# A four-layer graph network on one core: the deep slots of the first tile in units of their own, and gather rounds of four units

## What is computed

```python
# layer 0, twice: GAT, 4 heads of 32
h = (x @ W).reshape(N, H, C)
e = leaky_relu(alpha_s[src] + alpha_d[dst], 0.2)
e_exp = exp(e - segment_max(e, dst)[dst])
out = segment_sum(h[src] * (e_exp / segment_sum(e_exp, dst)[dst])[:, :, None], dst) + bias
# layer 1: weighted neighbour sum (edge weights), two dense branches
feat_neigh = segment_sum(edge_val[:, None] * feat_in[edge_col], edge_row)
# layer 2: graph transformer, 8 heads of 16, softmax over the edges of each node,
# two batch norms and a feed-forward part
w = einsum('ehd,ehd->eh', q[e_dst], k[e_src])
# layer 3: edge MLP with two batch norms over all edges, mean over each node's edges
e = (x_dst - x_src) @ theta_w.T + x_src @ phi_w.T
e = relu(_bn(e)); e = relu(_bn(e @ fc1_w.T))
x = relu(segment_sum(e, dst) / cnt + h)
```

## Time and profile before

| | us |
|---|---|
| median of 3 runs | 11876.77 (11870.55 to 11889.13) |
| the profiled execution | 11906.11 |
| its span | 11904.2 |
| PE busy | 3666.8 (31%) |
| DVE busy | 6743.4 (57%) |
| ACT busy | 1475.4 (12%) |
| POOL busy | 7495.3 (63%) |

### The profile page before, as it was taken

How to read it: one execution, slowest core, us unless ns; L and a number is a source line. 1 busy time by engine, 2 the same in 40 slices (tenths; PEclk the granted TensorE clock), 3 DMA queues, 4 the chain that set the end, 5 groups by cost and what they waited for, 6 DMA issues and landing times. The chain is left out here.

```text
span 11904.2 us, 90167 instructions
## 1 busy us (share of the span) xinstructions
PE 3666.8 (31%) x14212; PEld 2427.7 (20%) x14213; DVE 6743.4 (57%) x12448; ACT 1475.4 (12%) x2895; POOL 7495.3 (63%) x7840
## 2 busy tenths in 40 slices
PE   2212333332224555655000000005211111113987
PEld 1211222222112333433000000002111111112433
DVE  6455677774556777765556666655322222224877
ACT  1000111110000111111000000000000000002976
POOL 4676777775767777743677777770476777773023
PEclk7556666665567887877555555557555555556998
DMA  2255444453386667673374444450236433335866
GB/s 59 69 75 94 104 105 110 111 115 62 88 96 162 183 180 189 184 165 106 100 96 115 111 111 111 111 105 2 68 105 92 105 105 105 105 105 128 288 235 216
DMA packets 928522, 1422.47 MB, mean 119 GB/s; under 512 B 191108, under 2 KB 723306, under 8 KB 927992
## 3 DMA queue, kind: packets, MB, share of 16 engines
q0 software_dynamic: 277904, 662.94, 28.4%
q10 hardware_dynamic: 549664, 498.96, 14.6%
q1 hardware_dynamic: 100680, 257.93, 6.5%
HBM read 1064.18 MB, written 355.03 MB: 119 GB/s over the span
## 5 line engine op out<-in xcount | busy, mean ns | idle before, releaser
L819 POOL DMA_INDIRECT ring<-gat_table,index x3640 | 3475.2, 955 | 1261.6 <-issue 1046.9
L819 POOL DMA_INDIRECT ring<-b_table,index x1820 | 1734.2, 953 | 678.3 <-issue 526.0
L819 POOL DMA_INDIRECT ring<-kv_table,index x1820 | 1729.5, 950 | 601.4 <-issue 526.6
L961 PE MATMUL pairs<-hot_lo,hot_hi 128*128 128x128 f32 x6272 | 1089.5, 341 | 929.0 <-PEq L959 926.0
L961 PEld LDWEIGHTS pairs<-hot_lo,hot_hi 128*128 128x128 f32 x6272 | 1002.7, 246 | 1047.5 <-issue 1017.0
L1904 DVE TENSOR_TENSOR tb<-bt,att 128x1792 f32 x130 | 263.2, 2025 | 1676.1 <-DVEq L107 1676.1
L1926 PE MATMUL bt<-ident,ring 128*128 128x128 f32 x1820 | 417.4, 421 | 1945.5 <-PEq L107 1945.5
L954 PE MATMUL pairs<-nil 128*128 128x512 bf16 x784 | 328.9, 466 | 1918.3 <-PEq L107 1789.6
L935 DVE TENSOR_SCALAR hot_lo<-ramp,lo,col 128x128 f32<-128x128 f32 x3136 | 873.2, 355 | 0.0
L714 PE MATMUL tp<-ident,stage 128*128 128x128 f32 x196 | 49.0, 427 | 2460.2 <-DVEq L701 2426.0
L2059 ACT ACTIVATE r<-kept_ring,coef 128x448 f32<-128x448 f32 x1040 | 762.6, 758 | 190.5 <-ACTq L107 166.3
(11 more groups left out here) (410 smaller groups left out, 6879.9 us busy)
## 6 DMA issues: line engine op xcount, KB each, us to landing
kept_ring<-kept SPq DMA_DIRECT2D x260, 896.0 KB, 4.7
dense_weights<-dstage ACTq DMA_DIRECT2D x392, 512.0 KB
layer_out<-dense_weights ACTq DMA_DIRECT2D x98, 1568.0 KB
kept<-tb ACTq DMA_DIRECT2D x132, 896.0 KB, 3.8
ring<-gat_table,index POOLq DMA_INDIRECT x3640
ring<-kv_table,index POOLq DMA_INDIRECT x1820
ring<-b_table,index POOLq DMA_INDIRECT x1820
col<-turned ACTq DMA_DIRECT2D x400, 32.0 KB
```

What stands on the lines that cost most here:

```text
L819: pool.indirect_dma_start(self.ring[:, r * UG + i, :], None, self.table, bass.IndirectOffsetOnAxis(self.index[:, half, at:at + 1], 0)).the ...
L961: mm = pe.matmul(self.ps[:, b, i * P:(i + 1) * P], self.hot_hi[:, u, 4 * b + i, :], self.hot_lo[:, u, 4 * b + i, :], start=False, stop=Fal ...
```

## The change

The first band is only as deep as its tiles two to seven need. What the first tile has beyond that stands in *tail units* of 14 slots of that tile alone, ahead of the first band. `tail_units` reads their number, `tail_depth` the place in the slot tables where they begin. Every pass gains a loop over them with its own form of the computation (`tail_scores`, `tail_unit`, `tail_exponent`, and a `fold` in the mean). The total is rounded up to a multiple of four, and all loops go in rounds of four units. The slot tables are longer by the number of edges and split into four groups of 32 partitions instead of three. The diff, cut; the rest of it repeats these parts for the other consumers and renumbers their loops.

```diff
-SCOLS = UMAX * UG + 8 * CH * B7
-SPARTS = ((0, 44), (44, 88), (88, P))
+SCOLS = E + UMAX * UG + 8 * CH * B7
+SPARTS = ((0, 32), (32, 64), (64, 96), (96, P))
...
+            c(dve.tensor_copy(level[:, :], band[:, :]))
+            c(dve.tensor_reduce(level[:, 0:1], md[:, 1:B7], AX.X, ALU.max))
+
+            c(dve.tensor_scalar(bi[:, :], level[:, :], float(S - 1), None, ALU.add))
             c(dve.tensor_single_scalar(bi[:, :], bi[:, :], 1, ALU.arith_shift_right))
             c(dve.tensor_scalar(bcnt[:, :], bi[:, :], float(B7), None, ALU.max))
+            c(dve.tensor_scalar(tail[:, 1:2], bcnt[:, 0:1], float(S), None, ALU.mult))
+            c(dve.tensor_tensor(tail[:, 0:1], md[:, 0:1], tail[:, 1:2], ALU.subtract))
+            c(dve.tensor_scalar(tail[:, 0:1], tail[:, 0:1], 0.5 * (UG - 1), 1.0 / UG, ALU.add, ALU.mult))
+            c(dve.tensor_scalar(tail[:, 0:1], tail[:, 0:1], WHOLE, WHOLE, ALU.add, ALU.subtract))
+            c(dve.tensor_scalar(tail[:, 0:1], tail[:, 0:1], 1.0, None, ALU.max))
+            c(dve.tensor_copy(k.total[:, 5:7], tail[:, :]))
             c(dve.tensor_tensor_scan(run[:, :], k.ones[:, 0:NB], bcnt[:, :], 0.0, ALU.mult, ALU.add))
-            c(dve.tensor_scalar(ti[:, 0:1], run[:, NB - 1:NB], 1.0, None, ALU.add))
+            c(dve.tensor_tensor(run[:, :], run[:, :], tail[:, 0:1].broadcast_to([P, NB]), ALU.add))
+            c(dve.tensor_scalar(ti[:, 0:1], run[:, NB - 1:NB], float(RU - 1), None, ALU.add))
             c(dve.tensor_single_scalar(ti[:, 0:1], ti[:, 0:1], 2, ALU.arith_shift_right))
             c(dve.tensor_copy(k.total[:, 1:2], ti[:, 0:1]))
-            c(dve.tensor_scalar(k.total[:, 0:1], ti[:, 0:1], 4.0, 2.0, ALU.mult, ALU.add))
-            c(dve.tensor_scalar(k.total[:, 2:3], ti[:, 0:1], 2.0, 1.0, ALU.mult, ALU.add))
+            c(dve.tensor_scalar(k.total[:, 0:1], ti[:, 0:1], float(RU), None, ALU.mult))
+            c(dve.tensor_scalar(k.total[:, 2:3], ti[:, 0:1], float(RU // 2), None, ALU.mult))
...
+                if w == 0:
+                    c(dve.tensor_scalar(lone[:, :], ok, float(DUMMY), None, ALU.add))
+                    dve.sem_inc(lone_ready, 1)
...
+            depth = tail_depth(k, act)
+            act.wait_ge(cleared, 1)
+            for j, (lo, hi) in enumerate(SPARTS):
+                act.dma_start(slot_src[j][:, ds(band_chunks(act, 0) * CH, CH)], blank[lo:hi, 0:CH]).then_inc(lone_out, 16)
+            act.wait_ge(lone_out, 16 * len(SPARTS))
...
+                    if first:
+                        at = ((n - i - 1) * CH).with_bounds(min_val=0, max_val=SCOLS - CH)
+                        for j, (lo, hi) in enumerate(SPARTS):
+                            act.dma_start(slot_src[j][:, ds(at, CH)], lone[lo:hi, :]).then_inc(lone_out, 16)
...
-        last = self.rounds(pool)
-        round_(0)
-        with pool.Fori(0, last):
+        with pool.Fori(0, self.rounds(pool)):
+            round_(0)
             round_(1)
-            round_(0)
...
-    def load_index(self, sp, half, unit):
+    def load_index(self, sp, half, unit, depth):
         for j, (lo, hi) in enumerate(SPARTS):
-            sp.dma_start(self.index[lo:hi, half, :], self.slots[j][:, ds(unit * UG, 2 * UG)]
+            sp.dma_start(self.index[lo:hi, half, :], self.slots[j][:, ds(depth + unit * UG, 2 * UG)]
                          ).then_inc(self.i_sem[half], 16)
...
-        round_(0, 0, RU)
         with sp.Fori(0, last) as i:
+            round_(0, i, (RU * i + RU).with_bounds(min_val=0, max_val=UMAX))
             round_(1, i, (RU * i + RU + 2).with_bounds(min_val=0, max_val=UMAX))
-            round_(0, i + 1, (RU * i + 2 * RU).with_bounds(min_val=0, max_val=UMAX))
...
+            def tail_unit(u):
+                claim(dve, ga.landed)
+                got = ga.unit(u)
+                for f in tail_scores(dve, got, e_tail[:, 0:UG, :], work):
+                    c(f())
+                top = newmax[:, 0:heads]
+                c(dve.tensor_reduce(top, e_tail[:, :, :].rearrange("p s h -> p h s"), AX.X, ALU.max))
+                dve.tensor_tensor(x_tail[:, :, :], e_tail[:, :, :], top.unsqueeze(1).broadcast_to([P, UG + 1, heads]),
+                                  ALU.subtract).then_inc(e_ready, 1)
+                claim(dve, p_ready)
+                for half, dst in ((0, first), (1, second[:, :, :])):
+                    part = slice(half * B7, (half + 1) * B7)
+                    ins = dve.tensor_tensor(by_head(dst), by_head(got[:, part, 0:VB]),
+                                            p_tail[:, part, :].unsqueeze(3).broadcast_to([P, B7, heads, dim + 1]),
+                                            ALU.mult)
+                ins.then_inc(ga.used, 1)
+                c(dve.tensor_tensor(by_head(acc[:, 0:1, :]), by_head(acc[:, 0:1, :]),
+                                    p_tail[:, UG:UG + 1, :].unsqueeze(3).broadcast_to([P, 1, heads, dim + 1]), ALU.mult))
+                c(dve.tensor_tensor(first, first, second[:, :, :], ALU.add))
+                c(dve.tensor_reduce(second[:, 0, :], first.rearrange("p w c -> p c w"), AX.X, ALU.add))
+                c(dve.tensor_tensor(acc[:, 0, :], second[:, 0, :], acc[:, 0, :], ALU.add))
+                c.reset()
...
+                if isinstance(b, int):
+                    with dve.Fori(0, tail_units(k, dve)) as u:
+                        tail_unit(u)
...
+            with act.Fori(0, tail_units(k, act)):
+                tail_exponent()
...
+                    c(dve.memset(acc[:, 1, :], 0.0))
+                    with dve.Fori(0, tail_units(k, dve)):
+                        unit(1)
+                    claim(dve, tail.summed, 2)
+                    dve.sem_inc(tail.summed, 2)
+                    c(dve.tensor_reduce(fold[:, :], acc[:, 1, :].rearrange("p (w c) -> p c w", w=B7), AX.X, ALU.add))
+                    c.reset()
+                    dve.sem_inc(tail.folded, 1)
```

More of the change, by code:

```diff
@@ L512, in _, with band @@
                 act.sem_inc(turned_out[w], 32)
-            with act.Fori(0, NB) as b:
+            depth = tail_depth(k, act)
[3 more added lines that the diff above has]
+            act.wait_ge(lone_out, 16 * len(SPARTS))
+            act.sem_inc(lone_out, -16 * len(SPARTS))
+            def band(b, first):
                 n = band_chunks(act, b)
@@ L533, in _ @@
                     act.sem_inc(written, 1)
-            total = act.value_load(k.total[0:1, 0:1], min_val=2, max_val=UMAX)
-            act.wait_ge(cleared, 1)
+            band(0, True)
+            with act.Fori(1, NB) as b:
+                band(b, False)
+            total = act.value_load(k.total[0:1, 0:1], min_val=RU, max_val=UMAX)
             for j, (lo, hi) in enumerate(SPARTS):
-                act.dma_start(slot_src[j][:, ds(total * UG, 2 * CH)], blank[lo:hi, :]).then_inc(last, 16)
+                act.dma_start(slot_src[j][:, ds(depth + total * UG, 2 * CH)], blank[lo:hi, :]).then_inc(last, 16)
             act.wait_ge(last, 16 * len(SPARTS))
@@ L1176, in band @@
                 c.reset()
-            if by_source is None:
-                with dve.Fori(0, NB) as b:
-                    band(b, False)
-            else:
-                band(0, False)
-                with dve.Fori(1, NB) as b:
-                    band(b, True)
+            band(0, False)
+            with dve.Fori(1, NB) as b:
+                band(b, by_source is not None)
+            if by_source is not None:
                 for w in range(B7):
@@ L1894, in _, with units @@
             c.reset()
-            with dve.Fori(0, NB) as b:
-                c(dve.tensor_copy(att[:, :], at[:, ds(b * W7, W7)]))
-                c.reset()
-                u0 = band_start(k, dve, b)
-                with dve.Fori(u0, u0 + band_units(k, dve, b)) as u:
+            def units(first, n):
+                with dve.Fori(first, first + n) as u:
                     kept_unit = tb[:, ds(u % 2, 1)].rearrange("p r s c -> p (r s) c")
@@ L1928, in turn_units @@
                     mm.then_inc(turned, 1)
-            last = ga.rounds(pe)
-            turn_units(0)
-            with pe.Fori(0, last):
+            with pe.Fori(0, ga.rounds(pe)):
+                turn_units(0)
                 turn_units(2)
-                turn_units(0)
         @block.scalar
@@ L2113, in _ @@
                 last = source.rounds(pe)
-                for u in range(2):
-                    unit()
                 with pe.Fori(0, NB):
@@ L2159, in _ @@
                 c.reset()
-                for u in range(2):
-                    unit(u)
                 with dve.Fori(0, NB) as i:
@@ L2285, in _, with units @@
                 c.reset()
+                def units(first, n):
+                    with dve.Fori(first, first + n) as u:
+                        for j in range(S):
+                            source.dve_slot(dve, c, u, j)
+                            for h in range(2):
+                                c(dve.bn_stats(stats[:, 2 * j + h, :], source.e1[:, h, 0:QW]))
```

(20 more changed lines are left out.)

120 lines of the change are left out of this document (78 added, 42 removed).

## The result

The changed kernel takes 11240.92 us (median of 4 runs, 11233.11 to 11251.84), the kernel before 11876.12 us. The ratio is 0.9465, 95% interval 0.9452 to 0.9478: 635 us less, 5.3%. The forecast was 11258 us. A second set of runs beside later experiments gave 0.9467 (0.9454 to 0.9480).

A forecast was written before the change was run, and what follows sets the result against it. POOL's gather issue at 1.253 us each bounds the passes, except short stalls on dummy rows. 421 + 160 + 9 + 39 - 10 = 619 us off the 11876.8 us median gives 11258 us, range 11195 to 11340.

The forecast's parts named there:

- Units, 421 us: In all four passes: 6 units of 14 gathers go from each, 336 gathers at 1.253 us, 421 us less.
- Stalls, 160 us: End of the first band of each pass: POOL's waits on six dummy-heavy units go, 160 us less.
- ends, +9: Behind POOL's last gather: 7 us less in the first pass, 10 taken off for the second, 6 less in each other.
- Rival B: Two GAT passes: fewer dummies free ACT's held stores and DVE's idle time, 45 us more won, 11213 us; chance 0.16.
- Spread and mean, +39 us: Stages reading the kept units: six fewer units save 20 + 22 us, the mean's extra accumulator pass costs 3 us.
- Added work, -10 us: order_nodes 2 to 3 us, build_slots 6 us, register loads and index DMAs under 1 us each per pass: 10 us added.
- A: In the passes: stalls stay, from the tail unit's backlog plus dense rows' DMA or remaining dummy-heavy units; 11418 us, chance 0.10.
- C: In the passes: the index load becomes POOL's bound, slower than before, about 12990 us at 40 us a load; chance 0.02.
- cover of 33 us: In the passes: a pair's index is asked for 33 us before it is taken up, so a fourth index DMA is hidden.
- D: Whole kernel: the change doesn't do what it says, for example units don't fall because of rounding to four; 11887 us, chance 0.01.
- row on HBM pitches: Dummy gathers: a skill factor of 2 would give 82% DMA share, no POOL waits, a sum 160 us smaller; rejected for 3.3.

The follow-up runs named there:

- the cut alone: Kernel before with only its first band cut to 23 units, first tile's slots beyond 46 left out, 126 units in total: 11496.23 us, ratio 0.9662.

## Why the prediction was right, point by point

**Units, 421 us.** The counts came out at 3472, 1736 and 1736, and the pace at 1.25 us. The runs with 128 dummy rows show the term by itself: their passes differ by 102, 93, 104 and 105 us, 405 in all against 421. Twelve of the missing 16 us are the second pass, where DVE sets the end. The step stands.

**Stalls, 160 us, and ends, +9.** The stalls are gone, and the tail unit causes none. It lands as forecast, its first use on DVE standing at 446 us, 24 us after the first gather, where POOL has issued for 17.5:

```profile
445.98 0.27 DVE L1368 TENSOR_TENSOR es<-ring,ad 128x56 f32<-128x56 f32 x1 [26.66 <-DVEq L107]
```

Together the two terms were 169 us; the stages give 607 - 405 = 202 us, of which up to 19 can be the pair of executions. Both terms were mis-sized. Up to POOL's last gather the four passes lose 613 us, 192 more than the units' 421 and not 160. The 160 were counted around the end of the first band only; in the second pass POOL also waited 13 us between 5003 and 5071 and the 26.71 us of the earlier trace rows, together 39, and in the changed kernel it waits there once, for 3.4 us. Behind the last gather it is 2.6, -23.7, 7.2 and 8.4 us less, -6 in all and not +9. In the second pass the two belong together, since POOL now gets ahead of a DVE that sets the end. The forecast for that pass was 105 + 47 - 10 = 142 us, measured are 165. POOL's wait of 26.71 us went with the unit whose place in the ring it waited for, but DVE's idle time by ACT's held store did not go; here are ACT's queue and DVE in the changed kernel:

```profile
4953.55 24.09 ACTq L1042 DMA_DIRECT2D dense_weights<-dstage  x2
```
```profile
4985.79 1.12 DVE L1182 TENSOR_TENSOR first<-ring,first 128x924 f32<-128x924 f32 x1 [26.69 <-DVEq L107]
```

What went are smaller holds around it: in the kernel before DVE stood another 11.60 us in front of the unit at 5315.86 us, and ACT's store at 4981.51 us took 13.09 us, with DVE idle 14.99 us at 5002.90. That these make the other 23 us fits their size but was not tried by itself. Rival B (the holds of ACT go, 45 us) did not come true: the long hold stays, DVE's idle 18.38 us in the first pass became 7.90, and the two GAT passes gave 306 us where the forecast has 294. With 128 dummy rows the two stores take 1.57 us:

```profile
4956.27 1.57 ACTq L1044 DMA_DIRECT2D dense_weights<-dstage  x2
```

This is so in every run. The longest single issue of such a store is 24.8 us in the kernel before, 23.2 and 23.3 in the two runs of the changed one, 20.9, 36.5, 11.9 and 45.7 in the other four with one row, and at most 3.1 us in the six runs with four or 128 rows. So dummy reads cause the hold, by a queue that is not theirs. The first pass gave 141 us instead of 152. Seven of the 11 us are POOL's pace, which stalls left out is 1.263 us a gather there and was 1.259 (its rows are counted 958 ns in the mean instead of 955); why is open. The rest is the end, 2.6 us less and not 7.

**Spread and mean, +39 us.** Measured are 54 from the edge statistics on. The spread gave 28 us (452.0 to 423.9) and the mean 20 (477.2 to 457.3), against 20 and 19. The step that failed is that the tail unit costs the mean 3 us: over the whole it gives. DVE used to wait at the start of the mean for POOL's first initial sum, four operations from 11380.12 to 11390.43 us; the tail unit needs only a cleared accumulator and runs beside them. Before:

```profile
11388.36 2.07 POOL L2365 TENSOR_TENSOR acc<-acc,lift 128x896 f32<-128x896 f32 x1
...
11391.04 1.28 DVE L2358 SCALAR_TENSOR_TENSOR acc<-e,bound,acc 128x448 f32<-128x448 f32 x2 [20.98 <-DVEq L107]
```

and in the changed kernel:

```profile
10747.37 0.81 DVE L2586 MEMSET acc<- 128x896 f32 x1 [2.11 <-issue]
...
10755.62 0.68 DVE L2458 SCALAR_TENSOR_TENSOR acc<-e,bound,acc 128x448 f32<-128x448 f32 x1 [7.45 <-DVEq L107]
```

From the last statistics of the spread to the first sum of the mean it is 36.7 us before and 26.0 now, and 37.2 in the cut alone, which has no tail unit. Inside the mean the tail unit does cost: the cut alone has two units more and takes 457.7 us for the stretch that takes 457.3 here. Against this, 3.7 us more go by from the statistics to the spread (24.1 for 20.4) and 1.2 after the mean's last sum; the five differences make the 54.

**Added work, -10 us.** Measured are 3.4 us up to the first gather and 3.5 between the passes, -7.

**The sum.** 405 + 202 + 54 - 7 = 654 us by the two spans, against 619. The terms were off by -16, +33, +15 and +3 us; the medians lie 635 us apart, 19 less than this pair of spans. The mechanism was right; that the median came out 17 us from the forecast is in part luck, since misses of both signs cancel.

**The rivals.** A (stalls stay, 11418) falls: around the end of the first band POOL has no wait over 0.3 us in the first pass, and its pace of 0.8 gathers a microsecond in the others; its only other wait over 1.5 us inside a pass is the one of 3.4 us. C (the index load becomes the bound) falls: four loads in the kernel before cost 9 us in all, not 1736. The Trainium skill (DMA: Bandwidth & Descriptors, Anatomy of one DMA) gives a DMA about 2.0 us of fixed cost, fitted on DMAs issued from GpSimd, and these are issued by SP. POOL's waits at its claims are still 0.3 us (2.4 us for eight, above), so the load stays under its cover of 33 us; whether its four DMAs pay one after the other no run here shows. D falls by the counts, in spread and mean too (992 activations, 1040 before). The Trainium skill's row on HBM pitches that the prediction weighed (DMA: Bandwidth & Descriptors, Latency and other measured facts), a factor of 2 for rows at large strides, is not this case: the slow rows have no stride, with rows next to each other the slowness is gone, and with one row the factor was 3.3.

## What to carry to other kernels

Where an engine issues every gather at a fixed pace and waits for nothing, a pass costs its number of gathers times that pace, and padding costs as much as data; count the padding per tile from the inputs before looking for anything cleverer. Padding that points at one address costs more than its issue, and its price shows up elsewhere: in the landing of the last unit, and in another engine's stores. Spread it over a few rows (four took away 271 of 281 us in the passes here) before building code to avoid it: that alone was worth 265 us in the kernel before, and 70 us on top of the change.

## What was not expected of the hardware

Gathers in which nearly all of 128 rows are the same row came at about 75 rows a microsecond, whether the row had 512, 544 or 1088 bytes; at 1088 bytes that is 3.3 times the DMA time per byte of ordinary ones. Four distinct rows removed nearly all of it. What in the memory's path sets this rate no run shows. Stores of ACT's queue (512 kB each, issued beside such gathers) were held 24 to 26 us on their issuing engine for two, against 1.6 us without them. And an operation of DVE on 64x64 elements took 319 ns with its scalar from a tile and 219 ns with a constant.
